# Moving work between engines in the opening of a macaron block: norms to ScalarE, copies to VectorE, casts to GpSimd, stores to ScalarE's queue

## The chip, the cores and the metric

The kernel runs on the 8 cores of one Trainium2 chip. Every core gets two of the 16 sequences and a copy of all weights, and nothing is exchanged between cores. The metric is the device time in microseconds (us) of the slowest core. A core has TensorE (PE, matmuls), VectorE (DVE), ScalarE (ACT), GpSimd (POOL) and SyncE (SP, which here only issues DMAs). ScalarE can issue DMAs as well, from its own instruction stream.

## The reference

```python
x = x + 0.5 * _L0_ffn_ref(_layernorm(x), ...)
x = x + _L0_attn_ref(_layernorm(x), ...)
x = x + 0.5 * _L0_ffn_ref(_layernorm(x), ...)      # same weights as the first
```

`_L0_ffn_ref` with its fixed expert indices comes down to one product per token: `xn @ W_shared.T + g * (xn @ W_expert.T) + bias`, where g is the share of the two largest of seven softmax gates. They sum to one after normalising, so the kernel adds the two weights once and scales one product by a gate column. `_L0_attn_ref` is causal attention with 16 heads of 64, with Q, K, V and output projections of 1024x1024 and biases. x is 16 x 2048 x 1024 in float32; a core has 4096 rows of it.

## The kernel before

A core's 4096 rows are 32 tiles of 128 rows, in 8 chunks of 4 tiles (512 rows). Weights come from HBM as float32 pieces of 128x1024 (`("wl", j)`) and are made bfloat16: pieces 0 to 15 are summed in pairs (`("ws", j)`, into WF, the feed-forward weight), pieces 16 to 47 are cast one by one (`("wc", j)`, into WQKV and WP; 16 to 23 are Wq, 24 to 31 Wk, 32 to 39 Wv).

All engines walk the same list, ORDER, and each does the entries that are its own, in that order, with semaphores between them. The entries that matter here are, for layer norm l (0 before the first feed-forward, 1 before attention, 2 before the second feed-forward) and tile n:

- `("ld", n)` loads x; `("st", n)` or `("s1", n, h)` are the statistics (VectorE, BNS and MV)
- `("rt", l, n)` and `("r", l, i)`: the reciprocal deviation of a tile or of a chunk (ScalarE, LV and RS)
- `("a", l, n)`: the normalised tile, into XN, which has four buffers. It is VectorE's, except for the entries in the set ON_ACT, which ScalarE does by one ACTIVATE with scale and bias. For these `("rt", ...)` has two more small ACTIVATEs (NGM and NMR)
- `("t", l, n)`: XN transposed into XT1 or XT2. By TensorE into PSUM in the opening (with a copy from PSUM by ScalarE, or by VectorE for those in ON_DVE), by a DMA transpose that SyncE issues for later chunks
- `("ga", 0, i)` and `("gb", 0, i)`: the gates of chunk i; the matmuls of "ga" need all four transposed tiles of the chunk
- `("f", 0, n, h)`: half h of the feed-forward product of tile n, with its evacuation by VectorE into x; `("xf", 0, n)` adds the bias on GpSimd; `("sx", 0, n)` stores the result
- `("q", i, hp)`, `("k", i, hp)`, `("v", n, h)`: projections of chunk i. VectorE evacuates Q and K into QKS, which has four buffers; a buffer can be written again when its store to HBM has landed. `store_qk` (L748) and `store_v` (L755) store them, on ScalarE's queue for chunk 0 and on SyncE's queue for all others. GpSimd squares each QKS tile, for a bound on the scores; `("n", w, i)` sums the squares
- `("al", u)`: the three loads (Q, K, V) of an attention unit u; `("qd", k)`: a step of attention, with the exponentials on ScalarE and, on the diagonal, a mask product on VectorE (`("mk", k)`, L1226)

The opening is written out by hand in a_order: chunks 0 and 1 go through the first feed-forward, then chunk 0 through Q, K and V, then chunk 1. The first attention steps start in the middle of chunk 1's K. Chunk 3's norms and transposes (tiles 12 to 15) stand among chunk 1's V products, and its gates follow.

```python
ON_DVE = {("t", 0, 4), ("t", 0, 5)}

ON_ACT = {("a", 0, _n) for _n in range(4, 8)}
```

PSUM has 8 banks, handed out in turn in the order of the list (SHARED); when entries change places they may get other banks.

Of the kernel before, what the change touches and what calls it, by code (L numbers as in the profile page):

```python
# [74 lines left out]


def ffn_order(l, i):

    out = []
    for t in range(4):  # L80
        for h in range(2):
            out.append(("f", l, 4 * i + t, h))
        if t:
            out.append(("sx", l, 4 * i + t - 1))
    out.append(("sx", l, 4 * i + 3))
    return out
# [7 lines left out]
def a_order():  # L94
# [3 lines left out]
    cast = list(range(16, 40))  # L98
# [40 lines left out]
    for n in range(4):  # L139
        o += [("f", 0, n, 1), ("s1", n, 1), ("rt", 1, n)]  # L140
        one_cast()
        if n:
            o.append(("a", 1, n - 1))
            one_cast()
    o += [("f", 0, 4, 1), ("a", 1, 3)]
    one_cast()
    o += [("f", 0, 5, 1), ("t", 1, 0), ("f", 0, 6, 1), ("t", 1, 1), ("t", 1, 2)]
    one_cast()
    o += [("f", 0, 7, 1), ("t", 1, 3)]
    for i in range(NCHUNK):  # L150
# [64 lines left out]
        if i == 1:  # L215

            v = order[16:]
            for t in range(4):
                n = 8 + t
                o += [("f", 0, n, 0), ("f", 0, n, 1), ("sx", 0, n), ("rt", 1, n), v.pop(0), ("a", 1, n), ("t", 1, n)]  # L220
                o += [[("n", 1, 1), ("ld", 14)], [("b1", 1), ("ld", 15)],
                      [("b2", 1), ("rt", 0, 12), ("a", 0, 12), ("xf", 0, 12)],
                      [("st", 14), ("rt", 0, 13), ("a", 0, 13), ("xf", 0, 13)]][t]
            o += [v.pop(0), ("st", 15), ("rt", 0, 14), ("rt", 0, 15), ("a", 0, 14), ("xf", 0, 14), v.pop(0)]
            o += [("t", 0, 12), ("t", 0, 13), ("a", 0, 15), ("xf", 0, 15), v.pop(0), ("t", 0, 14), ("t", 0, 15)]
            o += [v.pop(0), ("ga", 0, 3), ("gb", 0, 3)] + ffn_order(0, 3)
        elif 2 <= i < 6:
            o += ffn_order(0, i + 2)
# [220 lines left out]

ON_DVE = {("t", 0, 4), ("t", 0, 5)}  # L450

ON_ACT = {("a", 0, _n) for _n in range(4, 8)}

# [16 lines left out]
_n = [0, 0, 0]  # L470
# [16 lines left out]
def build_program():  # L487
# [22 lines left out]
    with contextlib.ExitStack() as st:  # L510
# [161 lines left out]
        g_sq = sem("g_square")  # L672
        g_ot = sem("g_ot")

        def filled(e, entry):
# [83 lines left out]
        def gpsimd_program(e):  # L759
# [28 lines left out]
            for en in ORDER:  # L788
                if en[0] == "xf":
# [4 lines left out]
                    x = xtile(l, m)  # L794
                    e.tensor_tensor(x, x, BF[:, :], ALU.add).then_inc(g_b[l], 1)  # L795
                elif en in (("ws", 4), ("ws", 5)):
                    sum_pieces(e, en[1]).then_inc(g_ws, 1)
# [28 lines left out]
        def sync_program(e):  # L826
            for en in ORDER:
                if en[0] == "wl" and en[1] < 48:
# [16 lines left out]
                    elif prev >= 16:  # L845

                        e.wait_ge(a_wc, prev - 15)
                    e.dma_start(out=dst, in_=src).then_inc(d_wl[WSLOT[j]], 16)
# [7 lines left out]
                elif en[0] == "sx":  # L856
# [5 lines left out]
                    else:  # L862
                        e.dma_start(out=out[m * 128:(m + 1) * 128, :],
                                    in_=xtile(2, m)).then_inc(d_o[m % NXC], 16)
                elif en[0] in ("q", "k") and en[1]:
                    store_qk(e, en)
                elif en[0] == "v" and en[2] == 1 and en[1] >= 4:
                    store_v(e, en)
                elif en[0] == "al":
# [10 lines left out]
                    if u == 0:  # L880
                        e.wait_ge(a_wc, 24)
                    if PRED[u] >= 0:
# [27 lines left out]
                elif en[0] == "xl":  # L910
# [3 lines left out]
                    if m < 2:  # L914

                        e.wait_ge(a_wc, 31 + m)
                    if m < NXA:
# [12 lines left out]
        def tensor_program(e):  # L930
# [68 lines left out]
            def product(en, upto):  # L999
# [6 lines left out]
                if kind in ("q", "k"):  # L1006
                    i, hp = en[1], en[2]
                    w = int(kind == "k")
                    if not begin and hp == 0:
                        for t in range(4):  # L1010
                            transposed(e, ("t", 1, 4 * i + t))
                        if i == 0:
                            e.wait_ge(a_wc, 16 if w else 8)
                else:
                    n, h = en[-2], en[-1]
                    i, t = divmod(n, 4)
                if kind == "v" and n == 0 and h == 0 and not begin:
                    e.wait_ge(a_wc, 24)
                if kind == "p" and not begin:
                    if t == 0 and h == 0:  # L1020
                        e.wait_ge(d_ol[i % 2], 16 * (i // 2 + 1))
                    if n == 0 and h == 0:
                        e.wait_ge(a_wc, 32)
                for dc in range(begin, upto):
# [221 lines left out]
        def scalar_program(e):  # L1246
            nch = 0
            for en in ORDER:
# [24 lines left out]
                elif en in ON_ACT:  # L1273
# [4 lines left out]
                                 scale=RS[:, l, i % 2, t:t + 1]).then_inc(v_a[l], 1)  # L1278
                elif kind in ("q", "k") and en[1] == 0:
                    store_qk(e, en)  # L1280
                elif kind == "v" and en[2] == 1 and en[1] < 4:
                    store_v(e, en)
                elif kind == "wc":
                    j = en[1]
                    w, dc = divmod(j - 16, 8)
                    dst = WP[:, dc, :] if w == 3 else WQKV[:, w, dc, :]
                    if j == 32 or j >= 40:

                        e.wait_ge(a_wc, j - 16)
                    e.wait_ge(d_wl[WSLOT[j]], 16 * (WUSE[j] + 1))  # L1290
                    e.copy(dst, piece(j)).then_inc(a_wc, 1)
                elif kind == "r":
# [110 lines left out]
```

## Time and profile before

| | before |
|---|---|
| median of 3 runs | 1275.39 us (1274.25 to 1278.98) |
| the profiled execution | 1271.4 us |
| its slowest core's span (core 3) | 1269.8 us |
| spans of all cores | 1261.6 to 1269.8 us |
| PE, DVE, ACT, POOL busy on core 3 | 1160.9, 755.5, 743.1, 444.6 us |
| chain that ended last, by engine | PE 69%, DVE 12%, issue 8%, DMA 4%, ACT 3%, SP's queue 3% |

The profiled execution took 1.6 us more than its slowest core's span, and 4.0 us less than the median of the runs. Busy PE is 91% of the span, but in the first 320 us the core waits more than later: there TensorE, VectorE and the queues take turns in holding up the rest. A time in a row below is counted from the start of the core's span.

### The profile page before, as it was taken

Reading aid. Unit: us, or ns where it says so; the run is one execution under the profiler, and the core shown is the slowest. Engines: PE = TensorE matmul, PEld = TensorE weight load, DVE = VectorE, ACT = ScalarE, POOL = GpSimd, SP = SyncE. Lnnn points to the kernel's source line nnn. Section 1 sums busy time; section 2 is a strip of 40 time slices with the busy share of each in tenths; the row PEclk is TensorE's granted clock in tenths of the full one; section 3 lists DMA queues with packets and bytes.
Section 4 is the critical chain, followed back from the end, with each engine's and each line's share of the span. In section 5 each row is a group of like instructions: output and inputs, shape, how many; then the busy total and the mean of one; then the engine's idle time right before and its main releaser. Section 6 shows DMA issues by size and latency. Waiting matters only on the chain.

```text
span 1269.8 us, 28550 instructions; the slowest of 8 cores (1261.6 to 1269.8 us)
## 1 busy us (share of the span) xinstructions
PE 1160.9 (91%) x9038; PEld 434.3 (34%) x9038; DVE 755.5 (59%) x1366; ACT 743.1 (59%) x936; POOL 444.6 (35%) x310
## 2 busy tenths in 40 slices
PE   4779887997998999999899999999999999998987
PEld 2334332332332333333333333333333333333333
DVE  6674787777556455544645654556767564655555
ACT  3362133465666576777667556767666778776501
POOL 4422533245134204503421425434515061423242
PEclk9789899999999999999999999999999999999989
DMA  9979656597358437537443646756555664735152
GB/s 288 324 229 279 158 134 150 156 238 179 97 128 205 109 126 207 140 123 147 133 132 122 157 110 185 184 142 141 174 165 133 203 179 154 212 120 194 26 166 83
DMA packets 207302, 207.44 MB, mean 163 GB/s; under 512 B 127283, under 2 KB 172339, under 8 KB 207158
## 3 DMA queue, kind: packets, MB, share of 16 engines
q1 hardware_dynamic: 200256, 202.42, 58.6%
q10 hardware_dynamic: 6902, 3.20, 1.0%
q8 instruction: 78, 1.28, 0.4%
q14 instruction: 66, 0.54, 0.2%
HBM read 117.49 MB, written 67.11 MB: 145 GB/s over the span
## 4 chain that ended last, share of the span: by engine, by line
PE 69%; DVE 12%; issue 8%; DMA 4%; ACT 3%; SPq 3%; POOL 1%; DVEq 0%; ACTq 0%; POOLq 0%
PE PS L1039 42%; PE PS L983 10%; PE PS L960 10%; PE PS L991 4%; DVE PT L1226 2%; DVE BNS L1119 2%; DMA XC<-x 1%; PE PS L1103 1%; ACT PT L1338 1%; SPq L893 1%; DVE XN L1148 1%; DVE VST L1201 1%; DVE ATT L1226 1%; DVE QKS L1190 1%; DVE XC L1175 1%
## 5 line engine op out<-in xcount | busy, mean ns | idle before, releaser
L1338 ACT ACTIVATE PT<-PS,MB 128x1024 bf16<-128x1024 f32 (+3 forms) x428 | 401.4, 989 | 150.4 <-PE PS L960 150.2
L1039 PE MATMUL PS<-XT,WQKV 128*128 128x512 bf16 x1024 | 246.5, 386 | 8.4 <-DVE QKS L1190 3.5
L1039 PE MATMUL PS<-WF,XT 128*128 128x512 bf16 x1024 | 247.7, 387 | 3.4 <-DVE VST L1201 2.8
L813 POOL TENSOR_TENSOR SQ<-QKS 128x512 bf16<-128x512 bf16 x128 | 147.3, 1155 | 285.7 <-DVE QKS L1190 256.1
L1338 ACT ACTIVATE ATT<-PS,MB 128x1024 bf16<-128x1024 f32 x212 | 193.8, 965 | 63.3 <-PE PS L960 62.4
L820 POOL TENSOR_TENSOR OTT<-OS,RR 128x512 bf16<-128x512 f32 x64 | 82.2, 1284 | 378.9 <-ACT RR L1349 378.7
L960 PE MATMUL PS<-ATT 64*128 64x512 bf16 (+3 forms) x1280 | 180.3, 350 | 4.5 <-ACT PT L1338 3.5
L795 POOL TENSOR_TENSOR XC<-XC,BF 128x1024 f32<-128x1024 f32 x48 | 106.3, 2217 | 103.8 <-DVE XN L1148 103.8
L1039 PEld LDWEIGHTS PS<-XT,WQKV 128*128 128x128 bf16 x1024 | 92.1, 99 | 146.3 <-issue 53.9
L1039 PEld LDWEIGHTS PS<-WF,XT 128*128 128x128 bf16 x1024 | 92.7, 99 | 141.5 <-issue 49.9
L983 PE MATMUL PS<-PT,ATT 128*32 128x512 bf16 (+3 forms) x1712 | 119.6, 356 | 16.4 <-DVE PT L1226 16.3
L1039 PE MATMUL PS<-WQKV,XT 128*128 128x512 bf16 x512 | 124.8, 386 | 6.2 <-DVE VST L1201 5.1
L1175 DVE SCALAR_TENSOR_TENSOR XC<-PS,GG,XC 128x512 f32<-128x512 f32 x96 | 71.5, 748 | 78.2 <-PE PS L1039 77.0
L1119 DVE BATCH_NORM_STATS2 BNS<-XC 128x6 f32<-128x512 f32 x156 | 104.4, 688 | 15.5 <-DMA XC<-x 6.3
L960 PEld LDWEIGHTS PS<-ATT 64*128 64x128 bf16 x1280 | 47.6, 93 | 141.6 <-issue 139.5
L1347 ACT ACTIVATE RR<-PS 128x512 f32<-128x512 f32 x64 | 38.2, 597 | 97.3 <-PE PS L1103 96.6
L1201 DVE TENSOR_TENSOR VST<-PS,BV 128x512 bf16<-128x512 f32 x64 | 43.9, 688 | 73.4 <-PE PS L1039 69.1
L1226 DVE TENSOR_TENSOR PT<-PT,TRI 128x256 bf16<-128x256 bf16 x162 | 83.1, 552 | 5.3 <-ACT PT L1338 5.2
L1190 DVE TENSOR_SCALAR QKS<-PS,BQ 128x512 bf16<-128x512 f32 x64 | 47.7, 748 | 64.7 <-PE PS L1039 64.4
L1190 DVE TENSOR_SCALAR QKS<-PS,BK 128x512 bf16<-128x512 f32 x64 | 47.8, 748 | 59.5 <-PE PS L1039 54.5
L991 PE MATMUL PS<-PT,ONES 128*32 128x512 bf16 (+3 forms) x856 | 82.0, 351 | 0.0
L1148 DVE TENSOR_SCALAR XN<-XC,MV,RS 128x1024 bf16<-128x1024 f32 x76 | 75.3, 991 | 5.2 <-DMA XT<-XN 4.5
(104 smaller groups left out, 1050.9 us busy)
## 6 DMA issues: line engine op xcount, KB each, us to landing
XC<-x SPq DMA_DIRECT2D x30, 512.0 KB, 7.3
x1d<-XC SPq DMA_DIRECT2D x30, 512.0 KB, 4.7
XC<-x1d SPq DMA_DIRECT2D x18, 512.0 KB, 8.2
out<-XC SPq DMA_DIRECT2D x18, 512.0 KB, 3.3
ATT<-qd SPq DMA_DIRECT2D x64, 128.0 KB, 3.6
od<-OTT SPq DMA_DIRECT2D x64, 128.0 KB, 3.1
ATT<-kd SPq DMA_DIRECT2D x16, 512.0 KB, 5.7
ATT<-vd SPq DMA_DIRECT2D x16, 512.0 KB, 6.5
```

Source lines behind the costliest of these rows:

```text
L795: e.tensor_tensor(x, x, BF[:, :], ALU.add).then_inc(g_b[l], 1)
L813: e.tensor_tensor(SQ[:, m % 8, :], q, q, ALU.mult).then_inc(g_sq, 1)
L960: i = e.matmul(PS[:, S_BANK + 2 * m + h, off:512], kk[64 * h:64 * h + 64, (j + m) * 128:(j + m + 1) * 128], q[64 * h:64 * h + 64, off:512] ...
L983: e.matmul(PS[32 * g:32 * g + 32, O_BANK, off:512], vv[:, v + 32 * g:v + 32 * g + 32], ptile(k)[:, 2 * m + g // 2, off:512], start=(j + m ...
L991: i = e.matmul(PS[32 * g:32 * g + 32, D_BANK, off:512], ONES[:, 0:32], ptile(k)[:, 2 * m + h, off:512], start=(j == 0 and (m == 0 or c > 0 ...
L1039: m = e.matmul(sbank(en), a, b, start=(dc == 0), stop=(dc == DCN - 1))
L1119: m = e.bn_stats(BNS[:, b, 6 * h:6 * h + 6], xtile(l, n)[:, h * 512:(h + 1) * 512])
L1148: e.tensor_scalar(xn, xtile(l, n), MV[:, l, i % 2, t, 0:1], RS[:, l, i % 2, t:t + 1], ALU.subtract, ALU.mult).then_inc(v_a[l], 1)
L1175: i = e.scalar_tensor_tensor(x, sbank(en), GG[:, n // 4 % 2, n % 4:n % 4 + 1], x, ALU.mult, ALU.add)
L1190: was_read(e.tensor_scalar(QKS[:, m % NQK, :], sbank(en), bias[:, hp:hp + 1], None, ALU.add), en)
L1226: e.tensor_tensor(p, p, TRI[:, :].unsqueeze(1).broadcast_to([128, 2, 128]), ALU.mult).then_inc(v_mk, 1)
L1338: e.activation(ptile(k)[:, 2 * m:2 * m + 2, off:512], PS[:, S_BANK + 2 * m:S_BANK + 2 * m + 2, off:512], AF.Exp, bias=MB[:, u // HPN, hp % ...
```

## The change

Three entries `("a", 1, 0)` to `("a", 1, 2)` go from VectorE to ScalarE. The copies of the four transposed tiles of norm 1, chunk 0, go from ScalarE to VectorE. The casts of pieces 17, 19, 21 and 23 go from ScalarE to GpSimd. The stores of chunk 1's eight Q tiles go from SyncE's queue to ScalarE's. In the list itself the norms and transposes of norm 1, chunk 0, are placed anew, and chunk 3's transposes stand earlier.

```diff
+ON_POOL = (17, 19, 21, 23)
@@ a_order, after ws(7)
     for n in range(4):
         o += [("f", 0, n, 1), ("s1", n, 1), ("rt", 1, n)]
         one_cast()
-        if n:
-            o.append(("a", 1, n - 1))
+        if n < 3:
+            o.append(("a", 1, n))
             one_cast()
-    o += [("f", 0, 4, 1), ("a", 1, 3)]
+    o += [("f", 0, 4, 1), ("f", 0, 5, 1), ("t", 1, 0), ("t", 1, 1), ("a", 1, 3)]
     one_cast()
-    o += [("f", 0, 5, 1), ("t", 1, 0), ("f", 0, 6, 1), ("t", 1, 1), ("t", 1, 2)]
+    o += [("f", 0, 6, 1), ("t", 1, 2), ("t", 1, 3), ("f", 0, 7, 1)]
     one_cast()
-    o += [("f", 0, 7, 1), ("t", 1, 3)]
@@ a_order, chunk 1's V
-            o += [v.pop(0), ("st", 15), ("rt", 0, 14), ("rt", 0, 15), ("a", 0, 14), ("xf", 0, 14), v.pop(0)]
-            o += [("t", 0, 12), ("t", 0, 13), ("a", 0, 15), ("xf", 0, 15), v.pop(0), ("t", 0, 14), ("t", 0, 15)]
+            o += [("t", 0, 12), ("t", 0, 13), v.pop(0), ("st", 15), ("rt", 0, 14), ("rt", 0, 15), ("a", 0, 14), ("xf", 0, 14)]
+            o += [("t", 0, 14), v.pop(0), ("a", 0, 15), ("xf", 0, 15), ("t", 0, 15), v.pop(0)]
             o += [v.pop(0), ("ga", 0, 3), ("gb", 0, 3)] + ffn_order(0, 3)
@@
-ON_DVE = {("t", 0, 4), ("t", 0, 5)}
-ON_ACT = {("a", 0, _n) for _n in range(4, 8)}
+ON_DVE = {("t", 0, 4), ("t", 0, 5)} | {("t", 1, _n) for _n in range(4)}
+ON_ACT = {("a", 0, _n) for _n in range(4, 8)} | {("a", 1, _n) for _n in range(3)}
@@ waits for casts are split between two semaphores
+        def cast(e, j):
+            m = sum(p <= j for p in ON_POOL)
+            if j - 15 - m:
+                e.wait_ge(a_wc, j - 15 - m)
+            if m:
+                e.wait_ge(g_wc, m)
+        def cast_piece(e, j, copy):
+            w, dc = divmod(j - 16, 8)
+            dst = WP[:, dc, :] if w == 3 else WQKV[:, w, dc, :]
+            if j == 32 or j >= 40:
+                cast(e, j - 1)
+            e.wait_ge(d_wl[WSLOT[j]], 16 * (WUSE[j] + 1))
+            return copy(dst, piece(j))
@@ gpsimd_program
+                elif en[0] == "wc" and en[1] in ON_POOL:
+                    cast_piece(e, en[1], e.tensor_copy).then_inc(g_wc, 1)
@@ sync_program
-                elif en[0] in ("q", "k") and en[1]:
+                elif en[0] == "k" and en[1] or en[0] == "q" and en[1] > 1:
                     store_qk(e, en)
@@ scalar_program
-                elif kind in ("q", "k") and en[1] == 0:
+                elif kind == "k" and en[1] == 0 or kind == "q" and en[1] < 2:
                     store_qk(e, en)
```

VectorE before, in the opening, from the evacuation of tile 1's second half (L1175 evacuates a product, L1119 and L1122 are statistics, L1148 is a norm):

```order
L1175 SCALAR_TENSOR_TENSOR XC<-PS,GG,XC 128x512
L1119 BN_STATS BNS<-XC 128x6
L1122 BN_AGGR MV<-BNS 128x2
L1148 TENSOR_SCALAR XN<-XC,MV,RS 128x1024
...
L1175 SCALAR_TENSOR_TENSOR XC<-PS,GG,XC 128x512
L1148 TENSOR_SCALAR XN<-XC,MV,RS 128x1024
L1175 SCALAR_TENSOR_TENSOR XC<-PS,GG,XC 128x512
L1175 SCALAR_TENSOR_TENSOR PT<-PS,GG,PT 128x512 x2
L1190 TENSOR_SCALAR QKS<-PS,BQ 128x512
```

VectorE after the change, from the evacuations of tiles 4 and 5 (L1199 evacuates a product, L1167 copies a transposed tile, L1172 is a norm, L1214 evacuates Q):

```order
L1199 SCALAR_TENSOR_TENSOR XC<-PS,GG,XC 128x512 x2
L1167 COPY XT<-PS 128x8x128 x2
L1172 TENSOR_SCALAR XN<-XC,MV,RS 128x1024
L1199 SCALAR_TENSOR_TENSOR PT<-PS,GG,PT 128x512
L1167 COPY XT<-PS 128x8x128 x2
L1199 SCALAR_TENSOR_TENSOR PT<-PS,GG,PT 128x512
L1214 TENSOR_SCALAR QKS<-PS,BQ 128x512
```

Four norms between the evacuations have become one, and four copies have come in, of which the last two stand before the evacuation of tile 7.

ScalarE after the change, one of the three rounds that it now does in the same place (L1321, L1330: reciprocal deviation; L1327, L1333: the two small ones; L747 a cast; L1301 the norm):

```order
L1321 ACTIVATE LV<-MV 128x1
L1327 ACTIVATE NGM<-MV 128x1
L1330 ACTIVATE RS<-LV 128x1
L1333 ACTIVATE NMR<-NGM,RS 128x1
L747 CAST WQKV<-ATT 128x1024
L1301 ACTIVATE XN<-XC,NMR,RS 128x1024
```

Before, a round was the first and third of these and one or two casts, and the four copies of transposed tiles followed.

SyncE's queue before, at chunk 1's V and chunk 3's transposes (L755 is a V store, XT2 belongs to norm 1, XT1 to chunk 3):

```order
L893 DMA_TRANSPOSE XT2<-XN 128x8x128
L755 DMA vd<-VST 128x8x128
L893 DMA_TRANSPOSE XT1<-XN 128x8x128 x4
L755 DMA vd<-VST 128x8x128
```

SyncE's queue after the change, in the same place (L917 is a transpose, L777 a V store):

```order
L917 DMA_TRANSPOSE XT2<-XN 128x8x128
L917 DMA_TRANSPOSE XT1<-XN 128x8x128 x3
L777 DMA vd<-VST 128x8x128
L917 DMA_TRANSPOSE XT1<-XN 128x8x128
L777 DMA vd<-VST 128x8x128
```

Three of the four transposes now stand ahead of the V store instead of behind it.

## Rows read from the trace of the kernel before

**Rows 1.** Spans and mean granted clock of two cores.

```profile
core 1: 1268.9 us, clock 0.980
core 3: 1269.8 us, clock 0.979
```

**Rows 2.** Timeline, core 3, opening: start, us, engine, line, instruction, [idle before].

```profile
61.90 0.20 ACT L1304 ACTIVATE LV<-MV 128x1 f32<-128x1 f32 x1 [16.43 <-DVE MV L1122]
...
69.22 2.92 ACT L1291 CAST WQKV<-WP 128x1024 bf16<-128x1024 f32 x3
70.09 3.36 PE L1039 MATMUL PS<-WF,XT 128*128 128x512 bf16 x8
72.05 2.83 ACT L1272 COPY XT<-PS 128x1024 bf16<-128x1024 bf16 x3
...
76.98 5.30 PE L1039 MATMUL PS<-XT,WQKV 128*128 128x512 bf16 x16 [2.88 <-ACT XT L1272]
```

**Rows 3.** Timeline, core 3, around the first K product of chunk 1.

```profile
133.26 0.75 DVE L1190 TENSOR_SCALAR QKS<-PS,BQ 128x512 bf16<-128x512 f32 x1 [0.98 <-PE PS L1039]
...
140.00 1.34 SPq L748 DMA_DIRECT2D qd<-QKS  x3
...
145.31 1.41 DVE L1190 TENSOR_SCALAR QKS<-PS,BK 128x512 bf16<-128x512 f32 x2 [2.93 <-DMA qd<-QKS]
146.32 1.04 PE L1091 MATMUL PS<-SQ,BD 128*32 128x512 bf16 x8 [3.40 <-DVE QKS L1190]
```

**Rows 4.** Timeline, core 1, the same evacuation.

```profile
141.85 1.41 DVE L1190 TENSOR_SCALAR QKS<-PS,BK 128x512 bf16<-128x512 f32 x2 [1.04 <-DMA qd<-QKS]
```

**Rows 5.** Timeline, core 3, chunk 3's transposes and gates.

```profile
207.33 1.24 SPq L893 DMA_TRANSPOSE XT<-XN  x1
...
216.15 5.95 SPq L893 DMA_TRANSPOSE XT<-XN  x4
...
220.00 0.81 DVE L1148 TENSOR_SCALAR XN<-XC,MV,RS 128x1024 bf16<-128x1024 f32 x1 [4.47 <-DMA XT<-XN]
...
222.07 1.03 PE L1081 MATMUL PS<-WGT,XT 128*128 128x7 bf16 x24 [2.08 <-DVE VST L1201]
224.07 0.35 PE L1081 MATMUL PS<-WGT,XT 128*128 128x7 bf16 x8 [0.97 <-DMA XT<-XN]
```

**Rows 6.** Timeline, core 1, the same gates.

```profile
218.93 0.98 PE L1081 MATMUL PS<-WGT,XT 128*128 128x7 bf16 x24 [2.78 <-DVE VST L1201]
220.96 0.36 PE L1081 MATMUL PS<-WGT,XT 128*128 128x7 bf16 x8 [1.05 <-DMA XT<-XN]
```

**Rows 7.** Timeline, core 3, ScalarE's norm of a tile before the change.

```profile
35.16 0.19 ACT L1304 ACTIVATE LV<-MV 128x1 f32<-128x1 f32 x1
...
36.32 1.24 ACT L1277 ACTIVATE XN<-PT,NMR,RS 128x1024 bf16<-128x1024 f32 x1 [0.20 <-ACT NMR L1316]
```

**Rows 8.** The instructions of line L1143: duration in ns, min/median/max.

```profile
L1143 DVE COPY XT<-PS x2: 681/681/681, 37.3 to 37.9; 128x1024 bf16<-128x1024 bf16 x2
```

**Rows 9.** Groups of instructions by form, GpSimd: busy us, mean ns, idle before.

```profile
L795 POOL TENSOR_TENSOR XC<-XC,BF 128x1024 f32<-128x1024 f32 x48 | 106.3, 2217 | 103.8 <-DVE XN L1148 103.8
```

**Rows 10.** DMA issues, 33 to 39 us, core 3: count, size, us to landing.

```profile
WP<-wtq SPq DMA_DIRECT2D x4, 512.0 KB, 19.0
```

**Rows 11.** Timeline, core 3, VectorE and GpSimd, first 60 us.

```profile
17.21 2.97 POOL L795 TENSOR_TENSOR XC<-XC,BF 128x1024 f32<-128x1024 f32 x1 [0.69 <-DVE XN L1148]
18.12 2.60 DVE L1148 TENSOR_SCALAR XN<-XC,MV,RS 128x1024 bf16<-128x1024 f32 x1
...
59.95 0.75 DVE L1175 SCALAR_TENSOR_TENSOR XC<-PS,GG,XC 128x512 f32<-128x512 f32 x1 [2.60 <-PE PS L1039]
```

**Rows 12.** Window, core 3: us, PE, PEld, DVE, ACT, POOL busy, PEclk, DMA share, GB/s.

```profile
147.00:154.00 7.00, 7.00 (x36) 1.94 (x33) 5.17 (x8) 2.34 (x4) 5.71 (x5) 0.62 0.66 189
```

**Rows 13.** Waits of VectorE, core 3, 255 to 320 us: total, times, longest.

```profile
DVE BNS L1119 <- DMA XC<-x: 0.9, 1, 0.9
```

**Rows 14.** Waits of VectorE, core 1, 255 to 320 us.

```profile
DVE BNS L1119 <- DMA XC<-x: 3.4, 2, 2.5
```

More of the change, by code:

```diff
@@ L673, in build_program @@
         g_ot = sem("g_ot")
+        g_wc = sem("g_wcast")
         def filled(e, entry):
@@ L845, in sync_program @@
                     elif prev >= 16:
-                        e.wait_ge(a_wc, prev - 15)
+                        cast(e, prev)
                     e.dma_start(out=dst, in_=src).then_inc(d_wl[WSLOT[j]], 16)
@@ L880, in sync_program @@
                     if u == 0:
-                        e.wait_ge(a_wc, 24)
+                        cast(e, 39)
                     if PRED[u] >= 0:
@@ L914, in sync_program @@
                     if m < 2:
-                        e.wait_ge(a_wc, 31 + m)
+                        cast(e, 46 + m)
                     if m < NXA:
@@ L1012, in product @@
                         if i == 0:
-                            e.wait_ge(a_wc, 16 if w else 8)
+                            cast(e, 31 if w else 23)
                 else:
@@ L1017, in product @@
                 if kind == "v" and n == 0 and h == 0 and not begin:
-                    e.wait_ge(a_wc, 24)
+                    cast(e, 39)
                 if kind == "p" and not begin:
@@ L1022, in product @@
                     if n == 0 and h == 0:
-                        e.wait_ge(a_wc, 32)
+                        cast(e, 47)
                 for dc in range(begin, upto):
@@ L1282, in scalar_program @@
                     store_v(e, en)
[L1283 to L1291, printed above, removed]
+                elif kind == "wc" and en[1] not in ON_POOL:
+                    cast_piece(e, en[1], e.copy).then_inc(a_wc, 1)
                 elif kind == "r":
```

## Prediction, written before the changed kernel was run

> **What bounds the kernel now.** I looked at the spans of the cores first: they lie within 8 us, and core 3 and core 1 are the last [rows 1], so a gain counts only as far as both get it. Then the table of windows and the waits of TensorE, which show that the first 320 us wait most and the rest runs at a steady pace of TensorE and ScalarE. The edits all lie before 225 us, so I read the timeline of each engine at three places, to see there which wait ends last.
>
> *Place A, the end of the first feed-forward of chunk 0.* The first Q product starts at 76.98 us after an idle time of 2.88 us that ends with ScalarE's copy of the last transposed tile [rows 2]. ScalarE is late because it does three casts and then three copies in a row before that one (from 69.22 and from 72.05 us) [rows 2]. TensorE's last feed-forward product before it, eight matmuls in 3.36 us, and the first Q product run at the half clock of 1.2 GHz: 16 matmuls in 5.30 us is eight at 0.43 and eight at 0.23 us [rows 2].
>
> *Place B, the first K product of chunk 1.* Its evacuation starts at 145.31 us, after VectorE has sat idle for 2.93 us until a store of Q landed, and TensorE waits 3.40 us for the bank [rows 3]. That QKS tile had been evacuated at 134.0 us; its store was issued at 140.00 us [rows 3], because in SyncE's order the twelve loads of four attention units stand ahead of it. On core 1 the same wait is 1.04 us [rows 4].
>
> *Place C, chunk 3's gates.* TensorE waits 2.08 and 0.97 us before the two parts of the gate matmuls, on core 1 2.78 and 1.05 us [rows 5, 6]. Behind it is a chain: the norm of tile 15 waits 4.47 us for the transpose that frees its XN buffer, and that transpose is issued at 216.15 us although SyncE was done with the one before it at 208.57 us [rows 5]. It stood behind a V store.
>
> **The change part by part.**
>
> A, norms, copies and casts. VectorE loses three norms between evacuations, and so reaches tile 3's statistics sooner; but ScalarE's chain now decides. A round there is: from LV to the big instruction 1.16 us (35.16 to 36.32 us), which is now a cast; the cast, 0.95 us (2.92 us for three, less the overlap); the norm, 1.24 us less an overlap of 0.1 us [rows 2, 7]. That makes 3.25 us. The first LV is at 61.90 us [rows 2], so the fourth comes at 71.65 us, its RS 0.5 us later, and VectorE's norm of tile 3 is over at 73.1 us. TensorE transposes it until 73.9 us, VectorE copies it in 0.68 us [rows 8] after the copy of the tile before it, and is done at 75.1 us. Meanwhile TensorE has the last feed-forward product, which has moved behind the transpose: 1.9 us at full clock or 3.4 us at half, to 75.8 or 77.3 us. The copy is hidden by it, and Q starts there instead of at 76.98 us. Before, Q's first product then lost another 1.7 us to the half clock (3.43 against 1.72 us for eight). If only one of the two products meets the half clock, A gives 1.2 to 1.4 us at the end of the first Q product; if neither, 2.9 us; if both, -0.3 us. TensorE still has gaps of some 0.7 to 2.5 us before each transpose, so at least one slow stretch is likely. I take 1.7 us, range -0.3 to 2.9.
>
> The four casts on GpSimd: it has no such instruction in this trace. The nearest row is its addition of two tiles of the same width, 2.2 us [rows 9], as an upper bound; the lower is ScalarE's 0.95 us [rows 2]. I take 1.5 us. Pieces 20 to 23 are issued from 33 to 39 us and land 19.0 us later [rows 10], pieces 17 and 19 earlier, so the casts run between about 48 and 60 us, behind GpSimd's last addition of the opening, and nothing on TensorE needs them before 75 us. They cost nothing unless they hold up VectorE. That can be: a norm on VectorE at 18.12 us took 2.60 us, where an undisturbed one takes 0.81 [rows 5], while GpSimd's addition ran from 17.21 to 20.18 us, itself 0.75 us longer than its mean [rows 9, 11]. So the two shut each other out. VectorE's last two weight sums end at 57.35 us (59.95 less 2.60) [rows 11], beside the third and fourth cast. The margin is what VectorE idled behind them, 2.60 us, less the two matmuls that need the last sum, 0.5 us: 2.1 us. One cast of 1.5 us in the way fits, so I book 0; with two casts of 2.2 us in the way it would be 2.3 us. The Trainium skill has this as a rule (SBUF — State Buffer, Who interferes with whom): a VectorE instruction with two SBUF inputs shuts out a GpSimd instruction that reads SBUF, and the reverse, for its whole length. By that rule alone the sums would wait for a running cast, and the term would lie at 0 to 2.3 us instead of 0; the trace agrees with the shutting out [rows 11].
>
> B, the Q stores. ScalarE issues each store right after the evacuation; it has no work between the V stores of chunk 0 and the reciprocal deviation of chunk 2, and an issue takes it about what it takes SyncE, 0.45 us (1.34 us for three) [rows 3]. The store that mattered is issued at 134.1 instead of 140.00 us. If it lands 5.1 us after issue as before, that is 139.2 us, so the K evacuation is held by VectorE's own work alone and starts 2.9 us sooner on core 3, 1.0 us on core 1 [rows 3, 4]. The idle time of 3.40 us on TensorE shrinks with it, and behind it core 3 ran at 0.62 of the clock for 7 us [rows 12]; in them were 36 matmuls. VectorE was busy 5.17 of these 7 us, so I count 1.8 us of it as won on core 3, bounds 0 and 2.7 (0.38 x 7). B: 4.7 us on core 3, 1.0 us on core 1. The exponentials of the first step need the statistics of tile 11 and do not move; they come after the stores on ScalarE, and the stores wait for nothing later than Q's last evacuation, so nothing is queued in vain. The Trainium skill says (DMA: Bandwidth & Descriptors, Rules for kernel authors) that issuing from several engines shares the same 16 DMA engines and saves only issue time. That speaks against a faster store. The sum would be the same by it, since what is saved here is the place in the order of issue, 5.9 us.
>
> C, chunk 3's transposes. SyncE can issue tile 12's at 208.6 us, and it lands by 212.4 (3.8 us, as from 216.15 to 220.00) [rows 5]. Tile 15's norm then waits for nothing: VectorE does it where its wait began, at 215.5 us, 4.5 us sooner. Its transpose is issued at about 216.8 us, behind the one V store that still stands before it, and lands 3.1 us later (220.9 to 224.0) at 219.9 us, which is when TensorE is through with V (222.07 less 2.08). The gates start there, and both waits go: 3.1 us on core 3, 3.8 us on core 1 [rows 5, 6]. What is late next is V's last evacuation on VectorE, about level. Bounds 1 and 4 us.
>
> *Sum.* Core 3: 1.7 + 4.7 + 3.1 = 9.5 us, to 1260.3 us. Core 1: 1.7 + 1.0 + 3.8 = 6.5 us, to 1262.4 us [rows 1]. The slowest core goes from 1269.8 to about 1262.4 us. Further on the cores differ by chance: between 255 and 320 us core 1 waits 3.4 us for x tiles, core 3 0.9 us [rows 13, 14], and which core draws the bad lot may change. I allow 0.4 us for that: 1262.8 us, 7.0 us less than before. The profiled execution, 1271.4 us, becomes 1264.4 us; the median of the runs stood 4.0 us above it, so it becomes 1268.4 us.
>
> **The rivals.**
>
> *One place gives nothing or it is given back (0.34).* Either ScalarE's rounds leave TensorE so empty that both products of A meet the half clock, or the x tiles after 255 us, which all cores load at once, land late on every core now as on core 1 (2.5 us more [rows 13, 14]). For it: A's start of Q moves by only 1.2 us at best. Against: after 320 us nothing differs. A gone and 2.5 us lost there is 7.0 - 1.7 - 2.5: 2.8 us less, 1272.6 us.
>
> *Nothing arrives (0.09).* Another wait stands right behind each one removed: at C the V evacuation, at B the exponentials, which need tile 11's statistics either way. Then only core 3's excess goes, and core 1 stays: 1274.5 us.
>
> *More than the sum (0.09).* The slow stretches of the clock vanish at A and at C too, 1.7 us each: 3.4 us more, 1265.0 us.
>
> *Slower (0.04).* GpSimd's cast is slow. With D us each they run one after the other from about 49 us (an estimate, from the landings of [rows 10]); VectorE's two sums fall behind the second and third. At D = 4.4, twice the addition of [rows 9], the last sum ends at about 63.5 us instead of 57.35 us, TensorE stands 4 us, and with the clock that follows (1.7 to 3.4 us) the gain is gone. The first Q product also waits for the fourth cast, at 49 + 4 D; at D = 10 us that is 89 us, 12 us after 76.98 us, less the 5.3 us of B and C: 1282 us. It decides from about D = 8. No row shows GpSimd that slow on this width.
>
> The forecast itself has 0.44.
>
> **How the numbers follow.** A measurement of this kernel tells about 0.5% (6.4 us) from no change: 1269.0 us is the edge below. The forecast's own spread is about 3 us either way, as the bounds of A, B and C do not go wrong together, so some 0.3 of its 0.44 lies below the edge by itself; the rest of "faster" is the case of more (0.09) and the better part of the first rival, where only A's half is missing (0.13). Faster 0.52, slower 0.04 from its rival, within 0.5% the remaining 0.44. The range takes in the case of more and the case of nothing but leaves out the slow cast and the tails: 1262.5 to 1274.5 us.
>
> **What would show it.** The first Q product starting at 75.5 to 77.5 us on core 3, with no idle time on TensorE for a copy; GpSimd's casts of 1 to 2.2 us between 48 and 60 us and VectorE's first evacuation after them still at 60 us; K's first evacuation with no idle time for a Q store; the norm of tile 15 with no idle time for a transpose, and the gates right behind V. I am wrong if these waits are gone and the evacuation of the first product after the gates is not 6 us sooner, or if it is and the difference is lost by 320 us.

## The result and the profile after

| | before | after |
|---|---|---|
| median of 4 runs each | 1276.81 us (1274.25 to 1278.98) | 1266.32 us (1264.90 to 1266.66) |
| ratio, 95% interval | | 0.9922, 0.9900 to 0.9944 |
| the profiled execution | 1271.4 us | 1266.12 us |
| its slowest core's span | 1269.8 us (core 3) | 1264.6 us (core 7) |

The kernel is 0.8% faster. The forecast was 1268.4 us, 2.1 us above the median, and the range of 1262.5 to 1274.5 us holds it. The change was measured a second time with the experiments: 0.9938 (0.9917 to 0.9959). In some executions, whatever the kernel, the cores of one die ran at a lower mean clock and longer than the rest; the ratios leave out the slow ones, and the means of spans below leave out every execution with a core under 0.96 of the clock.

The spans of the cores after the change, the slowest three:

```profile
core 4: 1263.9 us, clock 0.981
...
core 6: 1263.5 us, clock 0.983
core 7: 1264.6 us, clock 0.983
```

*Place A.* The timeline of core 7 after the change, with ScalarE's round (LV to LV), the last transpose and the first Q product:

```profile
65.79 0.19 ACT L1321 ACTIVATE LV<-MV 128x1 f32<-128x1 f32 x1
66.89 1.05 ACT L747 CAST WQKV<-ATT 128x1024 bf16<-128x1024 f32 x1
67.85 1.24 ACT L1301 ACTIVATE XN<-XC,NMR,RS 128x1024 bf16<-128x1024 f32 x1
68.99 0.19 ACT L1321 ACTIVATE LV<-MV 128x1 f32<-128x1 f32 x1
...
73.45 1.65 PE L1086 MATMUL PS<-IDE,XN 128*128 128x128 bf16 x16
74.66 1.28 DVE L1167 COPY XT<-PS 128x1024 bf16<-128x1024 bf16 x2
74.94 1.89 PE L1063 MATMUL PS<-WF,XT 128*128 128x512 bf16 x8
76.66 3.62 PE L1063 MATMUL PS<-XT,WQKV 128*128 128x512 bf16 x16
```

A round takes 3.20 us. The last two copies (74.66 to 75.94 us) lie under the last feed-forward product, and Q follows it without a gap, where [rows 2] had 2.88 us; 16 matmuls of Q take 3.62 us instead of 5.30. The last feed-forward product and the first Q product ran at full clock on seven of the eight cores (on core 2 the former took 3.17 us for eight matmuls, at half). On core 3, for which the prediction gave 75.5 to 77.5 us, Q started at 73.92 us; 1.8 us of that is an opening that was sooner by as much (the evacuation of tile 0's second half at 58.13 instead of 59.95 us), and without it the start would be 75.7 us. GpSimd's casts on core 7:

```profile
48.78 1.03 POOL L747 CAST WQKV<-ATT 128x1024 bf16<-128x1024 f32 x1
51.45 1.04 POOL L747 CAST WQKV<-ATT 128x1024 bf16<-128x1024 f32 x1 [1.64 <-DMA ATT<-wtq]
54.79 1.04 POOL L747 CAST WQKV<-WP 128x1024 bf16<-128x1024 f32 x1 [2.29 <-DMA WP<-wtq]
57.60 1.34 POOL L747 CAST WQKV<-WP 128x1024 bf16<-128x1024 f32 x1 [1.77 <-DMA WP<-wtq]
```

And VectorE's last two weight sums and its next evacuation, which answer to [rows 11]:

```profile
55.68 1.22 DVE L727 TENSOR_TENSOR WF<-WQKV 128x1024 bf16<-128x1024 f32 x1
56.83 1.21 DVE L727 TENSOR_TENSOR WF<-ATT 128x1024 bf16<-128x1024 f32 x1
60.62 0.75 DVE L1199 SCALAR_TENSOR_TENSOR XC<-PS,GG,XC 128x512 f32<-128x512 f32 x1 [2.59 <-PE PS L1063]
```

On this core the sums were not held up, but the last cast was: it runs beside a sum and takes 1.34 us. On other cores both were. Core 0, its third cast:

```profile
55.95 1.57 POOL L747 CAST WQKV<-WP 128x1024 bf16<-128x1024 f32 x1 [3.08 <-DMA WP<-wtq]
```

And VectorE's two sums:

```profile
55.41 1.22 DVE L727 TENSOR_TENSOR WF<-WQKV 128x1024 bf16<-128x1024 f32 x1
56.54 2.06 DVE L727 TENSOR_TENSOR WF<-ATT 128x1024 bf16<-128x1024 f32 x1
```

On every core one of the four casts met a sum and took 1.18 to 2.01 us instead of 1.03 to 1.05, and on five cores (0 to 3 and 6) the last sum then took 2.06 instead of 1.22 us. That cost nothing: from the start of the first of these sums to the evacuation of tile 0's second half it is 4.94 us on core 0, as on core 3 before (4.95), because VectorE's idle time before that evacuation gave way. The Trainium skill's rule (SBUF — State Buffer, Who interferes with whom) would let a cast run only when the sum beside it has ended; the trace agrees, since on all eight cores the slowed cast ends 0.9 us after a sum (58.94 and 58.04 us on core 7), little less than the 1.03 us that it takes alone.

*Place B.* Core 7's first two K evacuations of chunk 1, which answer to [rows 3, 4], and SyncE's loads ahead of them:

```profile
127.45 0.33 SPq L909 DMA_DIRECT2D ATT<-qd  x1
...
133.25 0.83 SPq L879 DMA_DIRECT2D XC<-x  x2
...
143.27 0.75 DVE L1214 TENSOR_SCALAR QKS<-PS,BK 128x512 bf16<-128x512 f32 x1 [1.66 <-DMA qd<-QKS]
...
144.57 0.75 DVE L1214 TENSOR_SCALAR QKS<-PS,BK 128x512 bf16<-128x512 f32 x1 [0.55 <-DMA qd<-QKS]
```

The waits are smaller, not gone. The issues of core 7 from 133 to 141 us (count, size, median us from issue to landing) say why:

```profile
XC<-x SPq DMA_DIRECT2D x2, 512.0 KB, 9.8
qd<-QKS ACTq DMA_DIRECT2D x4, 128.0 KB, 7.7
```

The attention loads no longer stand behind the Q stores on SyncE. Their first is issued 1.87 us after the first Q evacuation of chunk 1 (125.58 us), where it was 6.07 us on core 3 before (127.06 and 133.13 us), and so loads and stores are in the DMA engines together. The store that the first K evacuation waits for, issued at 133.32 us, landed 9.7 us later.

*Place C.* Core 7's norm of tile 15 and its gates, which answer to [rows 5, 6]:

```profile
215.12 2.31 DVE L1172 TENSOR_SCALAR XN<-XC,MV,RS 128x1024 bf16<-128x1024 f32 x1
...
217.50 1.22 SPq L917 DMA_TRANSPOSE XT<-XN  x1
...
218.80 0.75 PE L1105 MATMUL PS<-WGT,XT 128*128 128x7 bf16 x24
...
220.69 0.34 PE L1105 MATMUL PS<-WGT,XT 128*128 128x7 bf16 x8 [1.14 <-DMA XT<-XN]
```

The norm waits for nothing, and the first 24 gate matmuls stand right behind V. The last 8 still wait, 0.6 to 1.15 us on the eight cores, because the norm of tile 15 ran beside a GpSimd addition and took 2.31 instead of 0.81 us. On the mean of the profiled cores the evacuation of the fourth gates comes 4.8 us sooner than before (217.3 instead of 222.1 us), and that of the fifth, near 315 us, 6.2 us sooner: nothing is lost again by then.

### The profile page after: what moved, and what is told of

Same layout as the page of the kernel before. It is cut to its first block, busy times and chain, and to the rows that moved or that the text cites. A ratio compares the mean times of both kernels' runs of the same rounds, so it can differ in the third digit from the quotient of the medians.

```text
span 1264.6 us, 28594 instructions; the slowest of 8 cores (1254.1 to 1264.6 us)
## 1 busy us (share of the span) xinstructions
PE 1155.7 (91%) x9038; PEld 434.0 (34%) x9038; DVE 757.4 (60%) x1367; ACT 740.1 (59%) x937; POOL 448.9 (35%) x314
## 4 chain that ended last, share of the span: by engine, by line
PE 66%; DVE 12%; issue 8%; DMA 6%; ACT 3%; SPq 3%; POOL 1%; DVEq 0%; ACTq 0%; POOLq 0%
PE PS L1063 40%; PE PS L1007 10%; PE PS L984 10%; PE PS L1015 4%; DVE PT L1250 3%; DMA XC<-x 2%; DVE BNS L1143 2%; PE PS L1127 1%; DMA qd<-QKS 1%; ACT PT L1355 1%; DMA ATT<-wte 1%; SPq L917 1%; DVE XN L1172 1%; DVE VST L1225 1%; DVE ATT L1250 1%
## 5 line engine op out<-in xcount | busy, mean ns | idle before, releaser
L1063 PE MATMUL PS<-XT,WQKV 128*128 128x512 bf16 x1024 | 243.1, 382 | 6.5 <-DVE QKS L1214 3.9
L1199 DVE SCALAR_TENSOR_TENSOR XC<-PS,GG,XC 128x512 f32<-128x512 f32 x96 | 71.5, 748 | 81.4 <-PE PS L1063 80.1
L1143 DVE BATCH_NORM_STATS2 BNS<-XC 128x6 f32<-128x512 f32 x156 | 104.4, 688 | 16.5 <-DMA XC<-x 7.4
L1214 DVE TENSOR_SCALAR QKS<-PS,BQ 128x512 bf16<-128x512 f32 x64 | 47.7, 748 | 61.0 <-PE PS L1063 60.7
L1214 DVE TENSOR_SCALAR QKS<-PS,BK 128x512 bf16<-128x512 f32 x64 | 47.9, 748 | 55.6 <-PE PS L1063 48.7
L1258 DVE CAST DSB<-PS 128x512 bf16<-128x512 f32 x64 | 44.2, 690 | 55.7 <-PE PS L1015 55.0
```

Source lines behind the costliest of these rows:

```text
L1063: m = e.matmul(sbank(en), a, b, start=(dc == 0), stop=(dc == DCN - 1))
L1143: m = e.bn_stats(BNS[:, b, 6 * h:6 * h + 6], xtile(l, n)[:, h * 512:(h + 1) * 512])
L1199: i = e.scalar_tensor_tensor(x, sbank(en), GG[:, n // 4 % 2, n % 4:n % 4 + 1], x, ALU.mult, ALU.add)
L1214: was_read(e.tensor_scalar(QKS[:, m % NQK, :], sbank(en), bias[:, hp:hp + 1], None, ALU.add), en)
```

## The experiments

Beside the ratio I use two finer readings. One is the mean of the eight cores' spans, over the executions of a kernel; its standard error is 0.3 to 0.5 us (0.9 for the kernel without the Q stores), where the slowest core depends on which core draws badly. The other is a table of stages from the profiled executions, each a mean over eight cores.

| kernel | ratio (95%) | mean of spans, less that of before |
|---|---|---|
| opening alone | 0.9999 (0.9982 to 1.0017) | 1267.3, -1.3 |
| Q stores alone | 0.9992 (0.9969 to 1.0014) | 1266.8, -1.8 |
| chunk 3 alone | 0.9974 (0.9949 to 0.9998) | 1264.7, -3.9 |
| all three, again | 0.9938 (0.9917 to 0.9959) | 1261.8, -7.0 |
| all but the Q stores | 0.9989 (0.9962 to 1.0017) | 1264.6, -4.2 |
| all but chunk 3 | 0.9977 (0.9959 to 0.9995) | 1265.6, -3.2 |
| all but the opening | 0.9962 (0.9929 to 0.9996) | 1263.7, -5.1 |
| all, loads behind K | 0.9960 (0.9937 to 0.9984) | 1264.0, -4.6 |
| all, last transpose late | 0.9963 (0.9946 to 0.9980) | 1263.9, -4.0 |
| all, three more casts on GpSimd | 0.9984 (0.9961 to 1.0007) | 1265.5, -2.4 |
| all, x loads sooner | 0.9939 (0.9917 to 0.9961) | 1261.7, -6.2 |
| all, with both edits | 0.9969 (0.9953 to 0.9984) | 1263.8, -4.1 |

Before had 1268.6, 1268.8 and 1267.9 us on the three chips: on the first ran the single parts and "loads behind K", on the second the next four of the table, on the third the last four.

Stages in us: f is the evacuation of tile 1's second-half product (the first expectation below counts from tile 0's, which is 1.8 us sooner), Q0 and Q1 the first Q evacuation of chunks 0 and 1, w the idle time of VectorE before the first three K evacuations of chunk 1, g the step from the evacuation of the third gates to that of the fourth.

| profiled execution | f to Q0 | Q0 to Q1 | w | g |
|---|---|---|---|---|
| before | 18.7 | 46.2 | 1.8 + 0 + 0.6 | 55.4 |
| opening alone | 16.3 | 47.3 | 4.0 + 0 + 1.2 | 55.7 |
| Q stores alone | 18.7 | 46.2 | 0.2 + 2.4 + 0 | 55.6 |
| chunk 3 alone | 18.8 | 46.5 | 2.7 + 0 + 1.2 | 52.8 |
| all but the Q stores | 16.4 | 47.7 | 3.3 + 0 + 0.9 | 52.8 |
| all but chunk 3 | 16.0 | 47.0 | 0.5 + 1.6 + 0 | 55.9 |
| all but the opening | 18.7 | 46.5 | 0.4 + 2.2 + 0.1 | 52.5 |
| all three | 16.3 | 47.3 | 0.3 + 0.7 + 0 | 52.6 |
| all, x loads sooner | 16.6 | 47.8 | 0 + 0.1 + 0 | 53.2 |

**The parts one by one.** Theory 1 was that the opening and chunk 3 carry the gain and the Q stores give nothing. Each kernel has one part of the diff and nothing else (the opening's own pieces, the norms, the copies, the casts and the order, were not taken apart any further but for the order, below); the first keeps the opening's, the second this, the third the two lines of chunk 3:

```diff
-                elif en[0] in ("q", "k") and en[1]:
+                elif en[0] == "k" and en[1] or en[0] == "q" and en[1] > 1:
                     store_qk(e, en)
```

> Only the opening's part of the change (norms on ScalarE, copies on VectorE, casts on GpSimd, their new order); Q stores of chunk 1 and chunk 3's transposes as in the kernel before. Theory 1 (the opening and chunk 3 carry the gain, the stores give nothing): from the evacuation of the first second-half product to that of the first Q product 17.7 to 18.1 us instead of 20.4 to 20.7, the rest as before: 2.6 us less, ratio 0.998. Rival (the parts add up to more than one sees alone, because each also takes away slow stretches of the clock): ratio 0.995 or lower. The prediction's own term was 1.7 us, ratio 0.9987.

> Only the stores of chunk 1's Q tiles on ScalarE's queue. Theory 1 (the loads of the four attention units no longer stand behind these stores, are issued some 6 us sooner and share the 16 DMA engines with the stores, so that the stores land 6 to 10 us after issue): ratio 0.999 to 1.001, an idle time for a Q store still there on VectorE before one of the first two K evacuations, on some cores. Rival (the prediction: the store lands 5.1 us after issue): the idle time of 1.0 to 2.9 us gone on all cores, ratio 0.9975 or lower.

> Only chunk 3's transposes placed sooner. Theory 1 (both waits of TensorE at the gates go and nothing takes their place): evacuation of the third to the fourth gates 53.4 us (51.8 on some cores) instead of 56.5 (54.8), 3.0 us less, ratio 0.9976. Rival (the core waits for its x tiles after 255 us instead): the same 3.0 us at the gates, and given back by 320 us, ratio 1.000.

The opening shows its 2.5 us at Q0 and little in the end; its ratio of 0.9999 misses the 0.998 of theory 1. The timeline of core 5, opening alone:

```profile
137.69 1.36 SPq L770 DMA_DIRECT2D qd<-QKS  x3
...
146.06 1.41 DVE L1214 TENSOR_SCALAR QKS<-PS,BK 128x512 bf16<-128x512 f32 x2 [6.06 <-DMA qd<-QKS]
```

Q is sooner there, but these stores, issued at 137.69 us behind the loads, took 8.0 us to land (median of three), and VectorE waits 6.06 us. The stores alone take away the first wait and get a second one, 2.4 us on the mean, as theory 1 has it. Chunk 3 alone gives its 2.7 us at the gates, and theory 1's ratio. This spoke for a theory 2: the opening and the Q stores only pay together. The four kernels below leave out one part or none:

> The changed kernel once more, with five rounds, beside the three kernels that each leave one part out. Theory 2, formed on the runs of the single parts (the opening and the Q stores only pay together: the opening alone ends 2.5 us sooner but VectorE then waits 4.0 instead of 1.8 us for the Q store; the stores alone move the wait by one evacuation, to 2.4 us; together the two waits are 1.0 us): ratio 0.992 to 0.995, on the mean of the cores 6.5 us less at the start of the third chunk's attention (367 instead of 373.5 us). Rival (the first measurement drew well and the parts add up to their sum, 0.35%): ratio 0.9965.

> The changed kernel with the stores of chunk 1's Q tiles back on SyncE's queue: the opening and chunk 3 alone. Theory 2: VectorE waits 4 us before the first K evacuation, as in the opening alone, the first two stages end where they ended before, and only the gates' 2.9 us stay: ratio 0.997 to 0.998. Rival (the parts are independent and the stores give nothing): ratio as the whole change, 0.992 to 0.994.

> The changed kernel with chunk 3's transposes where they stood before: the opening and the Q stores. Theory 2: both waits before K's evacuations together 1.0 us, the last K evacuation some 1.8 us sooner than before on the mean of the cores, the gates as before: ratio 0.997 to 0.9985. Rival (independent parts): the sum of the two alone, 0.999.

> The changed kernel with the opening as before: the Q stores and chunk 3. Theory 2: the second K evacuation waits 2.4 us as with the stores alone, the gates give 2.9 us: ratio 0.997 to 0.998. Rival (independent parts, the opening worth the 2.5 us that it shows): ratio 2.0 thousandths above that of the whole change, 0.994 to 0.996.

The waits are as theory 2 has them: without the opening, moving the Q stores changes the sum of w by +0.2 us (2.4 to 2.6) or, with chunk 3, by -1.2 (3.9 to 2.7); with the opening, by -3.1 and -3.2 us (5.2 to 2.1, 4.2 to 1.0). The times bear little of it out. The ratios of the four kernels are too wide to tell the theories apart, except that without the Q stores 0.9989 lies above theory 2 and far above the 0.992 to 0.994 of its rival, so the stores give something. On the mean of spans the single parts are worth 1.3, 1.8 and 3.9 us, in sum 7.0, and the whole change 7.0; left out of the whole, they are missed by 1.9, 2.8 and 3.8 us. A difference of two such means is uncertain by some 0.6 us (1.0 for the Q stores), so a bonus of 0.6 to 1.0 us for having both is possible, not shown. The kernel that has just these two parts (all but chunk 3) is 3.2 us below before, and its two parts alone are 1.3 and 1.8 us: no bonus there. "Only together" does not hold. One profiled execution per kernel also misled me: that of before has a mean span of 1266.2 us, 2.2 us under its mean over the executions of the three chips, 1268.4 us.

**The loads placed elsewhere.** If the stores land late because of the loads, other times for the loads must free them. The first five lines place them later (loads behind K), the lines below @@ sooner (x loads sooner):

```diff
+    move(("al", 1), ("q", 1, 7))
+    move(("al", 2), ("k", 1, 1))
+    move(("al", 3), ("k", 1, 3))
+    move(("ld", 12), ("k", 1, 2))
+    move(("ld", 13), ("k", 1, 4))
@@
+    move(("ld", 12), ("v", 2, 0))
+    move(("ld", 13), ("ld", 12))
@@
                 elif en[0] == "ld":
+                    if m in (12, 13):
+                        e.wait_ge(d_v[1], 16)
```

(`move` puts the first entry behind the second.)

> The changed kernel, with the loads of attention units 1, 2 and 3 and of x tiles 12 and 13 placed later in the list (behind Q 7, K 1, K 3, K 2 and K 4 of chunk 1), so that only one unit's three loads run beside the Q stores. Theory 1 (the stores land late because they share the DMA engines with 14 loads): the stores land some 2 us after issue, no idle time for a Q store on any core, and 1 to 2 us less than the changed kernel: ratio 0.991. Rival (a store issued by ScalarE lands late whatever else runs, or the idle time only moves to the exponentials or to the later loads): ratio 0.992 to 0.994, as the changed kernel or worse.

> The changed kernel with the loads of x tiles 12 and 13 issued when the second V store of chunk 0 has landed (near 123 us) instead of behind the twelve attention loads (near 133 us). Theory (the Q stores land late because the attention loads and the two x loads are in the DMA engines at the same time, and 124 to 128 us they are nearly idle): the Q stores land 2 to 5 us after issue, both waits before K's evacuations go (1.0 us in all on the mean of the cores), and unlike the placement behind K nothing collides with chunk 2's transposes: 1 to 1.5 us less on the mean of the cores. Rival (the attention loads alone keep the engines full, or start later behind the x loads): the same waits, no difference.

Later: the last five Q stores land in 1.9 us in the median on core 3 (the second to fourth, beside the one unit's loads, in 4.3 to 5.3), no core waits before a K evacuation, and the kernel is slower than the change, by 2.2 to 2.4 us on the mean of spans. The loads now meet chunk 2's transposes. Core 3's gates of chunk 2, loads behind K:

```profile
163.87 0.75 PE L1114 MATMUL PS<-WGT,XT 128*128 128x7 bf16 x24
...
168.82 0.34 PE L1114 MATMUL PS<-WGT,XT 128*128 128x7 bf16 x8 [4.21 <-DMA XT<-XN]
```

And the issues of the same core from 159 to 165 us:

```profile
XC<-x SPq DMA_DIRECT2D x1, 512.0 KB, 7.8
...
XT<-XN SPq DMA_TRANSPOSE x1, 8.9
```

The last transpose of chunk 2 lands 4.3 us after issue on core 7 of the changed kernel and took 8.9 us here; all eight cores wait for it at these gates, 1.6 to 4.2 us, where in the changed kernel four wait 0.9 to 1.1 us. Sooner: on core 0 the stores from 133 to 141 us land in 4.3 us, and seven of eight cores have no wait before K (core 3 one of 0.9 us). The cause of the late stores, loads and stores together in the engines, is shown both ways, and it is not ScalarE's queue: its stores land in 1.7 to 1.9 us once the loads are out of the way, and SyncE's took 8.0 us where the loads ran. The time stays that of the changed kernel, so the 1.0 us of waits that it still has is worth nothing that these runs can tell.

**The order at the end of the opening.** Last transpose late:

```diff
-    o += [("f", 0, 6, 1), ("t", 1, 2), ("t", 1, 3), ("f", 0, 7, 1)]
+    o += [("f", 0, 6, 1), ("t", 1, 2), ("f", 0, 7, 1), ("t", 1, 3)]
```

> The changed kernel with the last feed-forward product of the opening (tile 7's second half) ahead of tile 3's transpose again instead of behind it. Theory (the copy of the last transposed tile is hidden by that product, as the prediction has it): TensorE now waits some 1.2 us (0.5 for what is left of the copy of the tile before, 0.7 for the copy) between the last transpose and the first Q product, and the first Q product may meet the half clock; 1 to 3 us more from the first second-half evacuation to Q's, on the mean of the cores 1 to 2 us more than the changed kernel's 1261.8. Rival (the norms on ScalarE alone set the time, the order is free): the same 16.3 us and no difference.

Core 3 of this kernel:

```profile
73.52 0.61 PE L1086 MATMUL PS<-IDE,XN 128*128 128x128 bf16 x8
74.53 0.68 DVE L1167 COPY XT<-PS 128x1024 bf16<-128x1024 bf16 x1
75.56 4.69 PE L1063 MATMUL PS<-XT,WQKV 128*128 128x512 bf16 x21 [1.44 <-DVE XT L1167]
```

The copy is in the open, 1.44 us. f to Q0 is only 0.3 to 0.6 us longer (16.85 against 16.25 and 16.58 in the two profiled executions of the changed kernel), yet the mean of spans is 3.0 us less improved than the whole change's (2.2 us above the kernel with the x loads sooner, on the same chip); w is 2.0 instead of 1.0 us, and four cores take 55.3 to 55.8 us for g instead of 51.8 or 53.4. The hiding is confirmed; how 0.5 us grows to 2 or more is not settled.

**More casts on GpSimd.** TensorE waits for ScalarE's last Wk cast at the first K product of chunk 0, 1.47 to 1.90 us before (1.74 on core 3), 2.00 to 2.73 after.

```diff
-ON_POOL = (17, 19, 21, 23)
+ON_POOL = (17, 19, 21, 23, 27, 29, 31)
```

> The changed kernel with three more casts on GpSimd, pieces 27, 29 and 31 of Wk. In the changed kernel as before it TensorE waits 2.1 to 2.7 us at the first K product of chunk 0 for ScalarE's last Wk cast, and the half clock that used to fall on the first Q product falls there instead. Theory (half of what the opening wins is lost at that place): the wait goes, the stretch from the first Q evacuation of chunk 0 to that of chunk 1 is 2 to 3.5 us shorter (47.3 to about 44.5 us), and the mean of the cores is 1.5 to 3 us lower. Rival (the stretch is bound by the DMA engines, which are busy without a break from 92 to 124 us): the wait goes and VectorE waits as much longer for the store of a V tile; no difference. Slower if GpSimd's casts hold up VectorE's evacuations.

> The changed kernel with both edits: the three Wk casts on GpSimd and the two x loads sooner. If the two places are independent, the sum of what the two give alone (2.5 to 4.5 us on the mean of the cores, ratio 0.990 to 0.992); if the Q products reach chunk 1 sooner than the loads let them, only the larger of the two.

Both are misses, and neither theory named the reason. Core 3's GpSimd in this kernel:

```profile
86.59 1.04 POOL L747 CAST WQKV<-ATT 128x1024 bf16<-128x1024 f32 x1
87.59 2.93 POOL L837 TENSOR_TENSOR SQ<-QKS 128x512 bf16<-128x512 bf16 x2
90.46 1.03 POOL L747 CAST WQKV<-ATT 128x1024 bf16<-128x1024 f32 x1
```

And TensorE behind it:

```profile
91.64 5.09 PE L1063 MATMUL PS<-XT,WQKV 128*128 128x512 bf16 x16 [3.69 <-POOL WQKV L747]
```

Cast 31 stands behind the squares of two Q tiles on GpSimd and starts at 90.46 us; TensorE waits 3.69 us, and Q0 to Q1 grows from 47.3 to 49.9 us. With the x loads sooner as well, w is 0 on all cores and the ratio lies between those of the two. No version beat the changed kernel.

## Why the prediction was right

**Place A, 1.7 us booked (-0.3 to 2.9).** The steps held: a round of 3.20 us (3.25 forecast), the copy hidden under the last product, Q right behind it. The casts took 1.03 to 1.05 us alone, not 1.5; the one that met a sum took up to 2.01 us and held up the last sum by 0.84 us on five cores, and the margin of 2.1 us took that in: nothing lost, as booked. At Q0 the gain was 2.5 us, near the upper bound of 2.9 for the case in which neither product meets the half clock, and that case came true on seven cores: the slow stretch fell ahead of both products (between 66.7 and 74.7 us); over the executions the opening is worth 1.3 us alone and 1.9 us in the whole. The difference comes back before Q1. The windows of core 5 show where, before (us, busy times, then granted clock, DMA share, GB/s):

```profile
60.00:70.00 10.00, 7.82 (x51) 3.83 (x49) 9.18 (x16) 6.97 (x14) 0.00 (x0) 0.99 0.97 304
70.00:80.00 10.00, 7.11 (x30) 3.06 (x29) 2.99 (x5) 6.78 (x8) 0.00 (x0) 0.67 1.01 326
80.00:90.00 10.00, 10.00 (x48) 4.55 (x47) 9.06 (x18) 4.19 (x4) 4.16 (x4) 1.00 0.22 80
90.00:100.00 10.00, 8.10 (x44) 3.25 (x43) 7.47 (x9) 5.79 (x8) 5.81 (x6) 1.00 1.07 322
```

and after:

```profile
60.00:70.00 10.00, 6.58 (x39) 3.03 (x37) 8.18 (x15) 8.14 (x18) 0.00 (x0) 0.90 0.94 313
70.00:80.00 10.00, 9.47 (x53) 4.67 (x52) 6.62 (x11) 3.80 (x6) 1.29 (x2) 0.93 1.00 318
80.00:90.00 10.00, 8.67 (x41) 3.72 (x38) 8.94 (x16) 6.06 (x8) 5.90 (x6) 1.00 0.47 157
90.00:100.00 10.00, 9.25 (x41) 3.62 (x42) 6.22 (x8) 3.64 (x4) 4.15 (x4) 0.83 1.13 280
```

Summed over the windows, (1 - clock) x 10 us is 3.4 us in both. On this core the half clock has left the first Q product and taken the first K product instead, behind its wait for the cast. Core 3 before, where K's 16 matmuls ran at full clock behind that wait:

```profile
94.38 3.61 PE L1039 MATMUL PS<-XT,WQKV 128*128 128x512 bf16 x16 [1.74 <-ACT WQKV L1291]
```

Core 5 after:

```profile
90.75 5.30 PE L1063 MATMUL PS<-XT,WQKV 128*128 128x512 bf16 x16 [2.08 <-ACT WQKV L747]
```

Of the eight cores all lost 3.4 us in this way before; after, six lose 3.4 and two 1.7 us. Only three (2, 5 and 6) have the half clock at K (16 matmuls in 5.30 us); the others have it on feed-forward products and transposes before 75 us, between which TensorE waits for ScalarE's norms anyway (0.8 to 2.6 us at a time). Q0 to Q1 is 48.2 us on those three and 46.8 us on the other five, 46.2 before. The 0.5 us that all pay fits the longer wait for the cast: Q is sooner, ScalarE's last Wk cast is not by as much. My sum stopped at the end of the first Q product and so asked of two products only; the third, K's, had its own gap of 1.74 us in the trace of before.

**Place B, 4.7 us booked on core 3, 1.0 on core 1.** The step that failed is "If it lands 5.1 us after issue as before, that is 139.2 us". The store's earlier issue was right (133.32 us on core 7), its landing was 9.7 us behind, at 143.0 us. I had moved the stores out of SyncE's queue and not asked what then moves up in it: twelve loads, 4.2 us sooner. So the waits before K's evacuations fell from 2.4 to 1.0 us on the mean and did not go. The Q stores were worth 1.8 us alone and 2.8 us in the whole, inside my two figures; with the landing wrong, that is in part luck. The half clock behind the wait on core 3 did go, and with it the 1.80 us that VectorE idled there before the third K evacuation. No core of the changed kernel but core 4 idles over 0.1 us at that place, where four did over 0.9 us before; cores 4 and 7 still have a stretch at half clock from 145 or 146 us. The Trainium skill's rule (DMA: Bandwidth & Descriptors, Rules for kernel authors), that issuing from several engines saves only issue time, agrees with the trace: 128 KB stores issued by ScalarE took 7.7 us in the median where loads ran beside them, against 4.8 us (median of three) for SyncE's before and 8.0 us for SyncE's with the opening alone.

**Place C, 3.1 to 3.8 us.** The step between the gates is 2.8 us shorter on the mean, in the runs the part is worth 3.8 to 3.9 us. Right, but for the second wait, which I had gone and which stands at 0.6 to 1.15 us behind a norm of 2.31 us. I had the row for it, the norm of 2.60 us beside GpSimd's addition, and used it only for the opening.

**The sum and the rivals.** 7.0 us less was booked for the slowest core; the mean of spans fell by 7.0 us, the slowest core of the profiled executions by 5.2 us, and the two ratios make it 10.0 and 7.9 us of the median before. Booked in parts (1.7, 1.0 to 4.7, 3.1 to 3.8) and measured in parts (1.3 to 1.9, 1.8 to 2.8, 3.8 to 3.9) agree; that the sums agree to 0.1 us is luck, with an error of 0.6 us in the mean and a wrong step in B. "One place gives nothing" and "nothing arrives" fell: left out, each place is missed. The x tiles after 255 us, feared for all cores, waited at most 1.5 us on any core after. "More than the sum" is not needed, though the first median of 1266.32 us lies between its 1265.0 us and the forecast: a clock loss of 1.7 us vanished on two cores only in the profiled execution (on four in that of the second measurement). The slow cast fell at 1.04 us.

## What to carry to other kernels

When a transfer leaves a queue, list what stands behind it there: those transfers move up, and may collide with the one that was freed. When a gain rests on a clock stretch that goes away, look past the next product to the next gap of the engine; the same loss may wait there, as it did on three of eight cores. To rank edits worth 1 to 4 us of 1270, take the mean over all cores and executions, not one profiled execution and not the slowest core.

## What was not expected of the hardware

- Clock losses of TensorE from 60 to 100 us came in two sizes on every core of both kernels: 3.4 or 1.7 us.
- GpSimd casts 128x1024 from float32 to bfloat16 in 1.03 to 1.05 us, where ScalarE takes 1.05 us and where GpSimd's own addition of two float32 tiles of that width takes 2.2 us. Beside a VectorE sum of two such tiles the cast takes 1.18 to 2.01 us and ends 0.9 us after the sum; the next sum then takes 2.06 instead of 1.22 us and ends 1.08 us after the cast.
- A 128 KB store landed 1.73 us after issue ahead of the loads (core 3 before, issued at 132.35 us), 9.7 us beside attention and x loads; a transpose took 3.1 or 8.9 us. Which queue issued the stores made no difference that a run shows.
- VectorE's norm of 128x1024 takes 0.81 us alone and 2.31 us beside GpSimd's addition, which stays at 2.13 us.
